# A doubled stack load whose source is read twice, paired expert loads and a quartered Pool add, in a windowed attention and expert kernel

## What is computed

```python
qkv = einsum('bsi,oi->bso', x, w_qkv)            # split into q, k, v; 16 heads of 8
scores = q @ k.T / sqrt(8); allowed = (j <= i) & (i - j < 64)
x = layernorm(x + softmax(scores) @ v @ w_out.T + b_out)
logits = x @ gate_w + gate_b                      # top 2 of 8, softmax over the two
y_e = (silu(((x@w1+b1) * (x@w2+b2)) @ wg + bg)) @ w3 + b3
x = layernorm(x + sum_e weight_e * y_e)
```

## Time and profile before

| | us |
|---|---|
| median of 3 runs (lowest, highest) | 311.36 (309.72, 314.98) |
| the profiled execution | 311.95 |
| its span, first to last instruction | 310.2 |
| mean granted TensorE clock | 0.939 |

### The profile page before, as it was taken

The page is one execution under the profiler, slowest core; times in us unless marked ns, Lnnn a source line. Parts: engine busy times, 40 slices in busy tenths (PEclk is TensorE's granted clock), DMA queues, the critical chain, the costliest instruction groups (busy, mean ns, idle before and its releaser), DMA issues.

```text
span 310.2 us, 7675 instructions
## 1 busy us (share of the span) xinstructions
PE 237.9 (77%) x1791; PEld 174.1 (56%) x1791; DVE 217.2 (70%) x714; ACT 154.1 (50%) x410; POOL 161.0 (52%) x287
## 2 busy tenths in 40 slices
PE   2386579898979998887597878699999999995000
PEld 1155367676757777775355555566766766764000
DVE  6499537888878988886646677677777776774091
ACT  3636537868676968645125633244444334332043
POOL 6654002667666777777643662223464654656151
PEclk9999979999999999999679999999999999999555
DMA  4563425459686979766320112211111111100522
GB/s 119 181 157 91 137 75 143 128 149 273 195 249 189 281 203 268 181 202 240 113 60 3 36 53 68 78 37 51 42 56 32 51 40 45 48 18 7 201 104 101
DMA packets 33988, 36.50 MB, mean 118 GB/s; under 512 B 4972, under 2 KB 30062, under 8 KB 33824
## 3 DMA queue, kind: packets, MB, share of 16 engines
q1 hardware_dynamic: 30864, 29.69, 33.5%
q0 software_dynamic: 2336, 4.37, 4.3%
q10 hardware_dynamic: 752, 2.03, 2.0%
HBM read 25.48 MB, written 11.05 MB: 118 GB/s over the span
## 4 chain that ended last, share of the span: by engine, by line
PE 47%; DVE 14%; SPq 12%; issue 12%; DMA 8%; POOL 3%; ACT 2%; DVEq 0%; ACTq 0%; POOLq 0%
PE bank L1578 9%; PE bank L1550 8%; PE bank L1541 6%; SPq L409 5%; PE bank L1393 3%; DMA k_stack<-k_scratch 3%; PE bank L1573 2%; PE bank L1397 2%; PE bank L1566 2%; PE bank L1412 2%; DMA expert_out<-probs,tile_x 2%; DVE top L954 2%; SPq L422 2%; DVE shift L964 2%; DMA w_up<-expert_out 2%
## 5 line engine op out<-in xcount | busy, mean ns | idle before, releaser
L713 POOL DMA_INDIRECT expert_out<-probs,tile_x x39 | 40.3, 1034 | 58.2 <-DVE probs L1272 56.2
L813 ACT ACTIVATE probs<-bank 128x512 f32<-128x512 f32 x64 | 34.8, 592 | 20.0 <-PE bank L1397 19.6
L664 POOL DMA_INDIRECT routed<-rows,place x32 | 33.2, 1037 | 21.4 <-issue 16.5
L1578 PE MATMUL bank<-w_up,x_unit 128*128 x78 | 41.7, 617 | 0.0
L1550 PE MATMUL bank<-w_gate,x_all 128*128 x156 | 40.4, 382 | 0.5 <-DVE v_aug L1263 0.5
L1277 DVE TENSOR_TENSOR w_rows<-bank,b_up 128x512 f32<-128x512 f32 x39 | 26.8, 688 | 18.5 <-PE bank L1578 18.3
L964 DVE TENSOR_TENSOR shift<-top,delta_block 64x256 fp32r<-64x256 f32 x64 | 30.1, 471 | 11.9 <-PE bank L1397 9.5
L1541 PEld LDWEIGHTS bank<-w_down,xT 128*128 128x128 f32 x156 | 20.4, 190 | 31.2 <-issue 31.2
L888 ACT COPY x_unit<-bank 128x128 f32<-128x128 f32 x39 | 10.3, 264 | 55.3 <-PE bank L1558 55.1
L1393 PE MATMUL bank<-q_stack,k_stack 128*128 128x256 f32 x128 | 28.4, 305 | 10.9 <-issue 7.4
L954 DVE TENSOR_REDUCE top<-bank 128x4 f32<-128x384 f32 x64 | 33.5, 549 | 2.0 <-PE bank L1376 1.3
(11 more groups left out here) (177 smaller groups left out, 538.2 us busy)
## 6 DMA issues: line engine op xcount, KB each, us to landing
k_stack<-k_scratch SPq DMA_DIRECT2D x28, 160.0 KB, 3.2
q_stack<-q_scratch SPq DMA_DIRECT2D x62, 64.0 KB, 2.5
tile_x<-routed SPq DMA_DIRECT2D x39, 65.0 KB, 1.8
k_scratch<-k_parts SPq DMA_DIRECT2D x7, 320.0 KB
q_scratch<-q_parts SPq DMA_DIRECT2D x8, 256.0 KB
w_up<-in_L_ffn_w_dram SPq DMA_DIRECT2D x16, 128.0 KB
w_gate<-in_L_ffn_wg_dram SPq DMA_DIRECT2D x8, 256.0 KB
b_up<-in_L_ffn_b_dram SPq DMA_DIRECT2D x2, 1024.0 KB
```

What stands on the lines that cost most here:

```text
L664: eng.indirect_dma_start(routed, bass.IndirectOffsetOnAxis(ap=place[i][:, k:k + 1], axis=0), rows[i][:, k, :], None, bounds_check=SPARE + ...
L713: eng.indirect_dma_start(expert_out, bass.IndirectOffsetOnAxis(ap=tile_x[i][:, P:P + 1].bitcast(I32), axis=0), y[i][:, :], None, bounds_ch ...
L813: eng.activation(probs[t[1] % 2][a][:, 512 * h:512 * h + 512], t_bank[h][:, :], ACT.Exp).then_inc(probs_ready, 1)
L1578: eng.matmul(up_bank[:, :], tile_xT[n[1] % 2][:, :], of_expert(w_up, e[0])).then_inc(up_made, 1)
```

## The change

Five edits:

1. `q_stack` is laid out as [partition, hh, g, n] rather than [partition, g, hh, n], so the four g rows of a partition are one run of 4 KB in `q_stack` as well as in `q_scratch`.
2. `stack_queries` writes both copies at once: 4 transfers of 128 KB over 32 partitions. Its source is a hand-made access pattern whose first (outermost) dimension has step 0 and count 2. `stack_keys` likewise: 2 transfers of 320 KB over 64 partitions. `stacked` counts 96 per unit in place of 192. For unit 0 GpSimd issues one query transfer in place of two.
3. The matmul of `shifted_scores` reads the queries as four blocks of 64 that are 1024 elements apart, before 256 apart.
4. The loop loads the weights of two experts in each odd slot, four transfers of twice the size, in place of four in each slot.
5. GpSimd zeroes `q_stack[1]` in slot -2, before it waits for its own query transfer, and adds `b_out` in four instructions of 128 x 512, which wait for `k_lo` of unit 1.

```diff
-        POOL_PARTS = 2
+        Q_PARTS, K_PARTS = 4, 2
+        POOL_PARTS = 1
+        STACKED = 16 * (Q_PARTS + K_PARTS)
-        def stack_queries(eng, i, part):
-            hh, dup = part // 2, part % 2
+        def stack_queries(eng, i, hh):
+            held = q_scratch[i].rearrange("w (d h g) n -> h (w d) (g n)", d=HD, h=4)[hh]
             return eng.dma_start(
-                q_stack[i][64 * dup + hh:64 * dup + hh + 61:4, :, hh, :].bitcast(F32),
-                q_scratch[i].rearrange("w (d h g) n -> h (w d) g n", d=HD, h=4)[hh])
+                q_stack[i][hh:hh + 125:4, hh, :, :].rearrange("p g n -> p (g n)").bitcast(F32),
+                bass.AP(held.tensor, held.offset, [[0, 2], *held.ap]))
-        def stack_keys(eng, i, part):
-            return eng.dma_start(k_stack[i][32 * part:32 * part + 32, :, :].bitcast(F32),
-                                 k_scratch[i][part // 2].rearrange("(r g) n -> r g n", g=4))
+        def stack_keys(eng, i, w):
+            held = k_scratch[i][w].rearrange("(r g) n -> r (g n)", g=4)
+            return eng.dma_start(k_stack[i][64 * w:64 * w + 64, :, :].rearrange("p g n -> p (g n)").bitcast(F32),
+                                 bass.AP(held.tensor, held.offset, [[0, 2], *held.ap]))
-                    wait_apart(eng, wait_value, const_ready, stacked[i], pcount(later(u, -2), 192))
+                    wait_apart(eng, wait_value, const_ready, stacked[i], pcount(later(u, -2), STACKED))
-                    for part in range(8):
-                        if s != -2 or part < 8 - POOL_PARTS:
+                    for part in range(Q_PARTS):
+                        if s != -2 or part < Q_PARTS - POOL_PARTS:
-                        for part in range(4):
+                        for part in range(K_PARTS):
-                if s is None:
-                    e = t[0] * 4 + (t[1] - 4)
+                if s is None and t[1] % 2:
+                    e = t[0] * 4 + (t[1] - 5)
                     for c, w in enumerate((w1, w2)):
-                        eng.dma_start(w_up[:, bass.ds(e, 1), c, :],
-                                      w[bass.ds(e, 1)].rearrange("e h f -> h e f")).then_inc(experts_loaded, 16)
+                        eng.dma_start(w_up[:, bass.ds(e, 2), c, :],
+                                      w[bass.ds(e, 2)].rearrange("e h f -> h e f")).then_inc(experts_loaded, 16)
@@ gpsimd slot @@
-                if s == -1:
-                    eng.memset(q_stack[1][:, :, :, :].bitcast(F32), 0.0).then_inc(zeros_ready[1], 1)
                 if s == 1:
                     eng.wait_ge(loaded, 16 * 4)
-                    eng.tensor_tensor(x_all[:, :, :], x_all[:, :, :], bo[:, :].unsqueeze(1).to_broadcast([P, STEPS, P]),
-                                      ALU.add).then_inc(xb_ready, 1)
+                    eng.wait_ge(k_lo, 2)
+                    for q in range(4):
+                        held = x_all[:, 4 * q:4 * q + 4, :]
+                        eng.tensor_tensor(held, held, bo[:, :].unsqueeze(1).to_broadcast([P, 4, P]), ALU.add).then_inc(xb_ready, 1)
                 if s == -2:
                     eng.wait_ge(q_out, 16)
                     eng.wait_ge(zeros_ready[0], 1)
-                    for part in range(8 - POOL_PARTS, 8):
+                    for part in range(Q_PARTS - POOL_PARTS, Q_PARTS):
                         stack_queries(eng, 0, part).then_inc(first_stacked, 16)
+                    eng.memset(q_stack[1][:, :, :, :].bitcast(F32), 0.0).then_inc(zeros_ready[1], 1)
@@ residual @@
-                    eng.wait_ge(xb_ready, 1)
+                    eng.wait_ge(xb_ready, 4)
@@ shifted_scores @@
-                                   q_stack[i][:, grp, :, QT * w:QT * w + QT], start=(l == 0), stop=False,
+                                   q_stack[i][:, :, grp, QT * w:QT * w + QT], start=(l == 0), stop=False,
```

More of the change, by code:

```diff
@@ L483, in slot @@
                     eng.dma_start(routed[SPARE:SPARE + P, :], pad[:, :]).then_inc(spare_written, 16)
-                if s is None:
-                    e = t[0] * 4 + (t[1] - 4)
+                if s is None and t[1] % 2:
+                    e = t[0] * 4 + (t[1] - 5)
                     for c, w in enumerate((w1, w2)):
-                        eng.dma_start(w_up[:, bass.ds(e, 1), c, :],
-                                      w[bass.ds(e, 1)].rearrange("e h f -> h e f")).then_inc(experts_loaded, 16)
+                        eng.dma_start(w_up[:, bass.ds(e, 2), c, :],
+                                      w[bass.ds(e, 2)].rearrange("e h f -> h e f")).then_inc(experts_loaded, 16)
                     for held, w in ((w_gate, wg), (w_down, w3)):
-                        eng.dma_start(held[:, bass.ds(e, 1), :, :].rearrange("p e c n -> p (e c) n"),
-                                      w[bass.ds(e, 1)].rearrange("e (c p) n -> p (e c) n", p=P)).then_inc(experts_loaded, 16)
+                        eng.dma_start(held[:, bass.ds(e, 2), :, :].rearrange("p e c n -> p (e c) n"),
+                                      w[bass.ds(e, 2)].rearrange("e (c p) n -> p (e c) n", p=P)).then_inc(experts_loaded, 16)
                 if has(s, 4, STEPS - 1):
@@ L735, in _ @@
             eng.wait_ge(early_chain, EARLY_LINKS)
-            eng.wait_ge(experts_loaded, 16 * (4 * E + 4))
+            eng.wait_ge(experts_loaded, 16 * (2 * E + 4))
             run_end(piece, tile_slot)
@@ L1386, in shifted_scores @@
                 wait(eng, shift_ready, count(t, 4, 2 * a + 2))
-                wait(eng, stacked[i], pcount(u, 192))
+                wait(eng, stacked[i], pcount(u, STACKED))
                 for h in range(2):
```

## The result

The changed kernel takes 468.81 us (467.78 to 470.02, four runs) against 311.81 us before: a ratio of 1.507, 95% interval 1.498 to 1.516. It is slower by 157 us. The profiled execution took 470.02 us with a span of 468.2 and a mean granted clock of 0.798.

A forecast was written before the change was run, and what follows sets the result against it. Stack loop and engine work both bind. With two DMA engines, unit 0 at 38.4 us plus 7 x 31.3 puts unit 7 at 257.5; 177.6 more gives a span of 435.1, forecast 436 us, range 295 to 475.

The forecast's parts named there:

- The division by the outermost count: Stack transfers: a source whose outermost count is 2 is carried by two DMA engines, not sixteen; 23.9 us of data a unit.
- The rate: Stack transfers: each of the two engines moves 24.7 GB/s, 49.4 GB/s together.
- Unit 0: Its stack lands at 12.44 + 2.1 + 23.9 = 38.4 us rather than 21.6.
- After unit 7: From unit 7's first stack matmul to the end nothing changes: 177.6 us more.
- The loop: Attention units: landing to key store 4.65, to first query issue 0.7, landing 2.1, data 23.9; 31.3 us against 14.3 to 16.
- SP's issues: Stack issues on SP: six in place of twelve, 2.9 to 3.8 us a unit rather than 7.1.
- Pool's add: Unit 1: its split takes 3.26 us off the path; quarters cost 0 to 2 us with sixteen engines, nothing with two.
- The zeros moved on Pool: Before unit 0: the memset comes some 3 us earlier, with no effect on the time.
- Pairs of experts: Expert loads in the loop: bigger bursts taken as nothing, at most 1 to 2 us over the run.
- The rival of sixteen engines, faster: Stack transfers: sixteen engines carry them, the issue saving is real, 12 us gained, 299 us (294 to 305); chance 0.23.
- the rival that called the gain hidden: Attention units: with sixteen engines only the Pool part and a little idle time come off, 305 to 309 us; chance 0.11.
- the idle time before the stacks: TensorE before each unit's first stack matmul: idle 5.47 us once, then 1 to 2 us; 11.2 us over five units.

The follow-up runs named there:

- the version with sixteen engines: The changed kernel with the step of 0 as second dimension of the query source and keys stored in matching order: 308.5 us, ratio 1.002 to the kernel before.
- the run with quarters alone: The kernel before with only Pool's add in quarters behind the keys of unit 1, the memset where it was: 310.0 us, ratio 0.987.

## Why the prediction was right, and where its sizes were off

**The division by the outermost count** was right, and is now shown from three sides: a repeated source with 16 outermost is fast, an unrepeated one with 2 outermost is slow, and the cost follows the bytes on two engines. The rule of the Trainium skill (page "DMA: Bandwidth & Descriptors", sections "Why a DMA increments its semaphore by 16 and not by 1" and "Rules for kernel authors") said this in advance; the traces agree, with a share of 0.13 at 50 GB/s. The page's rule holds for any outermost dimension, with the zero-stride broadcast as its example; the padded scratch shows here that an ordinary outer dimension of 2 does the same.

**The rate** of 24.7 GB/s an engine was right: 50 GB/s for two.

**Unit 0** was put at 38.4 us and came at 40.5. **After unit 7** 177.6 was put and 178.0 measured.

**The loop** is the step that was mis-sized: 31.3 us predicted, 35.7 measured, which over seven units is 31 of the 33 us by which the span missed (435.1 against 468.2); unit 0 is the other 2. By its terms, as means over seven units: from landing to key store 5.13 us (4.65 put), store to first query issue 0.60 (0.7), first issue to next stack matmul 29.94 (2.1 + 23.9 = 26.0). So it is nearly all in the last one, where I had put the other traffic, and anything else, at nothing.

In unit 1, before any expert weights are loaded, that term is 27.8 us: 1.8 over. The windows at its start show where:

```profile
49.00:50.00 1.00, 1.00 (x10) 1.00 (x9) 1.00 (x1) 0.14 (x1) 1.00 (x1) 1.00 0.00 0
50.00:51.00 1.00, 1.00 (x17) 0.67 (x19) 0.94 (x3) 1.00 (x3) 0.16 (x1) 1.00 0.12 49
```

The first query transfer is issued at 45.16 us, but a steady flow on two engines begins only at 50.0, 4.8 us later, not 2.1; from there to the matmul at 72.96 it is 23 us at about 50 GB/s, close to the 23.9 us put for all the data. Why nearly nothing moves from 48 to 50 us is open. In the other six units the term is 28.7 to 31.2 us. With the expert weights out of the loop it is 28.2 in the mean of the first six units, where the change has 29.75, so between 1.1 and 1.6 us of it are expert weights: unit 1, which loads none, differs by 0.5 too. How the rest divides was not measured. The other traffic is the likely part. The page has the stores of the next unit's queries, which are issued while the two engines work:

```profile
q_scratch<-q_parts SPq DMA_DIRECT2D x8, 256.0 KB, 19.4
```

They land 19.4 us after their issue (median), where the version with sixteen engines has 2.2. So whatever is issued behind the stacks waits about as long as they do, and the two engines carry its sixteenths as well. The key stores, issued when the two are free, still landed in 2.3 us.

**SP's issues** fell as said: 0.53 to 0.61 us a query issue. The key issues took 0.9 to 2.0 us each rather than 0.49; that SP waited at full queues is likely but not shown. Either way it is hidden behind the data.

**Pool's add** was right in its cause and its own size, and unseen under the 28 us of data, as said. Without that cover, in the run with quarters alone, the two `spread_top` take 0.87 us in place of 4.13, and unit 1 comes 4.6 us sooner; the 1.3 us beyond the 3.3 were not looked into. The quarters made two later pairs of `spread_top` take 2.12 and 1.96 us in place of 0.87 each, 2.3 us together, just over the 0 to 2 us put.

**The zeros moved on Pool** were put at nothing, and that step failed. I followed Pool's own queue and the wait of SP, and didn't ask which VectorE instructions the memset would now lie beside. It costs 3 us on VectorE; no run shows what it costs in the total, since putting the memset back gave no gain (308.9 against 307.0). The row of the kernel before couldn't show it, since there the memset lay beside maxima, which read PSUM, and `spread_top` pairs that stayed at 0.87 us.

**Pairs of experts** were put at nothing to 2 us: 314.2 against about 312, which can't be told from nothing, with the late tokens as its mechanism.

**The rival of sixteen engines, faster (299 us)** would have been wrong even had the division been otherwise. The version that has its conditions, with one key store more a unit, took 308.5, which is the forecast of the rival that called the gain hidden (305 to 309). The idle time before the stack matmul did fall, from 11.2 to 5.9 us, and unit 1 came 3 us sooner. But units 2 to 6 last 14.9 to 16.6 us though TensorE is idle before their stacks for at most 0.7 us, and 2.6 us before unit 7. That the engines' own work takes about as long as the stack loop, as the 14.3 us of unit 5 had said, explains why little is gained, but not all: from unit 2 to unit 7 this version takes 78.5 us and the run with quarters alone 79.3, where the kernel before takes 75.8. Part of the lead is lost, and how is not shown. I had counted the stall of the first unit as gained for good. In the run with quarters alone the granted clock is 0.91 in the stretches from 60 to 80 and from 120 to 140 us, where the kernel before has 1.00 from 60 to 140. But the version that keeps sixteen engines has 1.00 there too and loses its lead all the same, so the clock can't be the whole cause. I had also read the idle time before the stacks as 1 to 2 us a unit; in the earlier trace rows it is 0.6 us or less from unit 5 on, so there was less to gain in the later units than I wrote.

## What to carry to other kernels

Before two transfers are joined into one, look at the outermost dimension of both sides: a count of 2 there took the transfer off fourteen of the sixteen DMA engines, whether the dimension repeated a source or was only a seam that no longer joined. Put a factor of 16 outermost and the repetition inside, even if the layout of both operands has to follow. In a profile the sign was idle engines beside a DMA share that stayed at 2/16. And when an instruction is moved on Pool, read what VectorE does in its new place, not only who waits for it.

## What the runs showed that was not expected

A memset on Pool holds up some VectorE instructions and not others. The cast from float32 to fp32r, both in SBUF, took 3.47 us beside it instead of 0.42, about as long as the memset lasted. `spread_top` with two SBUF operands kept its 0.87 us a pair beside the memset in the kernel before, but took 4.13 beside the add, which reads SBUF. The Trainium skill, page "SBUF — State Buffer", section "SBUF: two separate sides", tells these apart: a VectorE instruction in a fast mode with two ports and any Pool instruction shut each other out, the one that starts first going first, and a VectorE instruction with two SBUF inputs is in conflict only with a Pool instruction that reads SBUF. The traces agree on both (the memset began at 15.75 and the cast at 16.10, the add at 22.38 and the `spread_top` at 23.55), if the cast runs in such a mode, which no run here tested.

A padding of four rows in DRAM cost 63 us (375.0 against 312.3) with nothing else changed; against the kernel before of their own groups the two ratios are 1.195 and 1.010.
